# Computing only the chosen expert of each token, from lists in DRAM, in a two-layer decoder on one core

## The chip, the cores and the metric

One Trainium2 chip, one NeuronCore. The metric is the device time of one launch in microseconds (us), median of several runs. The engines are TensorE (PE: matmuls and transposes), VectorE (DVE), ScalarE (ACT), GpSimd (POOL) and SyncE (SP, which here only issues transfers). Each runs its own instruction list in order and waits on semaphores for the others.

## The reference

Two decoder layers on x of shape (16, 512, 256) in float32. Each sublayer is added to x after a layer norm. Layer 0 is a gated linear scan over the sequence, a cross attention with 16 heads on 64 context tokens, and a dense sublayer. Layer 1 is a positional attention whose parameters come from an LSTM over the sequence, a second cross attention, and this mixture of experts, the sublayer that the change is about:

```python
logits = jnp.einsum('bsd,ed->bse', x, w_router)          # 8 experts
indices = jnp.argmax(softmax(logits), axis=-1)
onehot = jax.nn.one_hot(indices, NUM_EXPERTS)
h = jnp.einsum('bsd,ehd->bseh', x, w_fc)                 # 256 -> 128 for each expert
h = jnp.where(h >= 0, h, 0.5 * h)
h = h * h
out = jnp.einsum('bseh,edh,bse->bsd', h, w_proj, onehot) # 128 -> 256
```

Each of the 8192 tokens uses one expert of eight.

## The kernel before

The work is cut into units of 128 positions of 4 sequences (512 tokens, `NT`): 4 chunks of positions by 4 groups of sequences, 16 units for each layer. A kernel-long schedule has six stages. Stages 0 and 1 run two units of layer 0 side by side in each body (2 bodies each; stage 1 has 64 LSTM steps in a body beside them). In stages 2 and 3 each of 4 bodies has one unit of layer 0, one of layer 1 (a chunk two behind) and 32 LSTM steps. In stage 4 a body has a unit of layer 1 and 32 LSTM steps, in stage 5 a unit of layer 1 alone.

The order of instructions on each engine is written by a planner at build time (`planned`). It lists the steps of each stream (`layer0_steps`, `layer1_steps`, `lstm_steps`) with a cost and what each needs, and places them one by one. LSTM steps have due times: in a body of stage 2, 3 or 4 the 32 of them are spread over 128, 140 or 112 of the planner's units (`PACE`). In stages 0, 4 and 5 (`WARM`) it fills nine tenths of each gap that it plans for PE with matmuls whose result nobody reads ("warm": bf16, 128x512), which keep PE busy. The planner decides the order alone; the real time of a step is the chip's.

An LSTM step is a loop over three engines: `gates` on PE, tanh on ACT, three small operations on DVE, tanh on ACT, the new state and its transpose on DVE, and then the next `gates`.

The expert part of a unit is computed densely. After the last norm, PE computes the router's 512x8 logits (`router` 0), DVE and ACT find each token's expert, PE turns the one-hot (`router` 4), and then for each of the 8 experts: `hidden` on PE (two 128x128 by 128x512 matmuls), ReLU on ACT, `leaky` on DVE, `select` on PE (spreads the one-hot of this expert over partitions), `kept` on DVE (multiplies by it), Square on ACT, and `expert` on PE (four 128x128 by 128x256 matmuls that add into two PSUM banks). `x6` adds the sum to the residual and SP stores the unit to `out`. The weights of all experts (`wfc`, `wpj`) are loaded once at the start.

## Time and profile before

| | us |
|---|---|
| median of 3 runs | 3078.72 (3077.14 to 3085.44) |
| profiled execution, its own time | 3086.61 |
| its span, first to last instruction | 3084.7 |
| PE busy | 2724.8 (88%) |
| DVE busy | 2042.3 (66%) |
| POOL busy | 1045.9 (34%) |
| ACT busy | 932.5 (30%) |

In the span, the share of busy time of an engine is a mean over stages with different limits. The store of a unit to `out` marks the end of each layer-1 unit. By these stores the stages take: start and stages 0 and 1 708 us, stage 2 683, stage 3 687, stage 4 529, stage 5 473. "Interval" below is the time between two such stores. In the profile an fp32 matmul counts as two instructions. PE's granted clock (PEclk) is a mean share of full speed. The trace names the DRAM copies of x and its norm `x_dram` and `xln_dram`.

### The profile page before, as it was taken

How to read it: one execution, taken by the hardware profiler on the slowest of the kernel's cores; microseconds unless marked ns; L12 is line 12 of the kernel's file. 1: busy time of each engine (PE TensorE's matmuls, PEld its weight loads, DVE VectorE, ACT ScalarE, POOL GpSimd, SP SyncE). 2: the span in 40 equal slices, each digit the busy share in tenths (PEclk: the TensorE clock that was granted, in tenths of full speed). 3: DMA queues.
4: the chain of work that ended last, by engine and by line, in shares of the span. 5: the costliest groups of instructions: out<-in, count | busy, mean ns of one | idle time of the engine just before them, and what ended most of it. 6: DMA issues, size and time to landing. Idle time of an engine off the chain costs nothing.

```text
span 3084.7 us, 38068 instructions
## 1 busy us (share of the span) xinstructions
PE 2724.8 (88%) x11733; PEld 1591.8 (52%) x11733; DVE 2042.3 (66%) x6490; ACT 932.5 (30%) x2361; POOL 1045.9 (34%) x956
## 2 busy tenths in 40 slices
PE   5799897886888988897988889898999998999999
PEld 2465554352555555463645555554555554555555
DVE  3576776887878696867778696866475664434433
ACT  0133233242324233332423233332322332222222
POOL 0254432332525242513425242513141340422422
PEclk9899897897899899888888999998999998999999
DMA  5210201001010101101010101000011010110100
GB/s 173 68 50 14 64 1 50 1 28 60 15 52 15 53 14 39 35 12 48 26 48 14 59 14 38 22 27 28 29 34 34 14 35 28 42 41 16 53 27 8
DMA packets 127166, 110.37 MB, mean 36 GB/s; under 512 B 31234, under 2 KB 126039, under 8 KB 126624
## 3 DMA queue, kind: packets, MB, share of 16 engines
q1 hardware_dynamic: 127008, 108.55, 11.4%
q8 instruction: 64, 1.05, 0.1%
q14 instruction: 94, 0.77, 0.1%
HBM read 76.81 MB, written 31.72 MB: 35 GB/s over the span
## 4 chain that ended last, share of the span: by engine, by line
PE 40%; issue 26%; DVE 23%; POOL 8%; ACT 2%; SPq 1%; DMA 1%; POOLq 0%; DVEq 0%; ACTq 0%
PE p L687 4%; PE p L781 4%; PE p L842 4%; PE p L854 4%; PE p L744 4%; PE p L720 3%; DVE l_xnat L1049 3%; DVE uin L1278 3%; PE p L681 3%; PE p L698 3%; PE pg L753 2%; PE p L734 2%; POOL l_scratch L1360 2%; DVE ln_stats L1024 2%; DVE l_scratch L1075 2%
## 5 line engine op out<-in xcount | busy, mean ns | idle before, releaser
L1348 POOL TENSOR_TENSOR l_kbd<-l_kg,headmask 128x512 f32<-128x512 f32 x256 | 265.4, 1047 | 376.7 <-PE p L720 277.4
L1334 POOL TENSOR_TENSOR ln_rstd<-ln_ve,neghalf 128x4 f32<-128x4 f32 x96 | 97.9, 1020 | 863.5 <-DVE ln_ve L1033 862.9
L1278 DVE SCALAR_TENSOR_TENSOR uin<-gates 16x20 f32<-16x20 f32 x512 | 185.7, 363 | 215.2 <-ACT gates L879 212.3
L1355 POOL TENSOR_TENSOR l_scratch<-l_scratch,l_mx 128x512 f32<-128x512 f32 x256 | 266.7, 1046 | 148.7 <-DVE l_mx L1079 147.9
L744 PEld LDWEIGHTS p<-l_vg,l_scratch 128*128 128x128 f32 x2048 | 266.1, 202 | 95.8 <-DVE l_xnat L1092 37.9
L879 ACT ACTIVATE gates<-pg 16x80 f32<-16x80 f32 x512 | 115.2, 225 | 650.7 <-PE pg L753 649.5
L720 PE MATMUL p<-l_kbd,l_qT 128*128 128x512 f32 x512 | 282.9, 642 | 22.5 <-DVE l_scratch L1075 21.8
L744 PE MATMUL p<-l_vg,l_scratch 128*128 128x34 f32 x2048 | 278.2, 285 | 17.7 <-DVE l_xnat L1092 9.5
L761 PE MATMUL p<-warm 128*128 128x512 bf16 x1077 | 286.8, 395 | 0.0
L842 PE MATMUL p<-l_xT,wfc 128*128 128x512 f32 x512 | 283.4, 647 | 1.1 <-DVE hr L1232 1.0
L854 PE MATMUL p<-wpj,hq 128*128 128x256 f32 x1024 | 264.9, 387 | 8.5 <-ACT hq L955 8.5
L681 PE MATMUL p<-ident,l_xnat 128*128 128x128 f32 x1024 | 188.1, 316 | 86.8 <-DVE l_xnat L1049 84.8
L753 PE MATMUL pg<-wcat,slots 128*16 128x80 f32 x1024 | 170.6, 252 | 93.6 <-DVE slots L1290 91.6
L854 PEld LDWEIGHTS p<-wpj,hq 128*128 128x128 f32 x1024 | 187.0, 190 | 91.1 <-issue 59.2
L753 PEld LDWEIGHTS pg<-wcat,slots 128*16 128x16 f32 x1024 | 58.1, 96 | 335.6 <-DVE slots L1290 167.4
L681 PEld LDWEIGHTS p<-ident,l_xnat 128*128 128x128 f32 x1024 | 133.8, 160 | 167.2 <-DVE l_xnat L1049 127.8
L1075 DVE TENSOR_TENSOR l_scratch<-p,l_neg 128x512 f32<-128x512 f32 x256 | 174.4, 683 | 49.0 <-PE p L720 43.9
L908 ACT ACTIVATE l_scratch<-p 128x512 f32<-128x512 f32 x256 | 149.4, 591 | 136.5 <-PE p L734 135.4
L890 ACT ACTIVATE l_xT<-p 128x512 f32<-128x512 f32 x192 | 105.6, 593 | 269.9 <-PE p L681 269.1
L734 PE MATMUL p<-ident,l_scratch 128*128 128x128 f32 x1024 | 169.2, 294 | 17.7 <-POOL l_scratch L1360 6.1
L882 ACT ACTIVATE pg<-pg 16x20 f32<-16x20 f32 x512 | 72.3, 141 | 371.4 <-DVE pg L1281 369.6
L903 ACT ACTIVATE l_scratch<-l_scratch 128x512 f32<-128x512 f32 x256 | 159.1, 622 | 76.2 <-POOL l_scratch L1355 75.6
(166 smaller groups left out, 4762.4 us busy)
## 6 DMA issues: line engine op xcount, KB each, us to landing
xln<-xln_dram SPq DMA_DIRECT2D x40, 512.0 KB, 3.9
l_vg<-v_dram SPq DMA_DIRECT2D x32, 544.0 KB, 3.9
l_kg<-k_dram SPq DMA_DIRECT2D x32, 256.0 KB, 4.2
xln_dram<-l_xnat SPq DMA_DIRECT2D x16, 512.0 KB, 3.0
x_dram<-l_xres SPq DMA_DIRECT2D x16, 512.0 KB, 4.1
l_xres<-x_dram SPq DMA_DIRECT2D x16, 512.0 KB, 3.7
out<-l_xres SPq DMA_DIRECT2D x16, 512.0 KB, 2.9
xin<-in_x SPq DMA_DIRECT2D x12, 512.0 KB, 3.8
```

Of the source, the lines that this page charges most:

```text
L681: i = pe.transpose(banks[l][m][:, b * P:(b + 1) * P], src[:, b, m * P:(m + 1) * P], ident[:, :])
L720: pe.matmul(banks[l][j], w.qT[:, j, b * P:(b + 1) * P], w.kbd[b % 2][:, j, :, :].rearrange("p a k -> p (a k)"), start=True, stop=True).the ...
L734: i = pe.transpose(t_bank[l][:, p * P:(p + 1) * P], src, ident[:, :])
L744: i = pe.matmul(o_bank[l][:, q * VW:(q + 1) * VW], w.exT[:, j, p, :], w.vg[:, b, q * VW:(q + 1) * VW], start=True, stop=True)
L753: pe.matmul(pg[0:B, 0:80], slots[:, s % STEPS, :], wcat[:, :], start=True, stop=True).then_inc(l_pe, 1)
L761: pe.matmul(pg[:, :] if layer == 0 else banks[0][0], warm[:, 0:P], warm[:, :], start=True, stop=True)
L842: i = pe.matmul(banks[1][2 + i_ % 2], wfc[:, k, i_ * P:(i_ + 1) * P], tiles[1].xT[:, k, :], start=(k == 0), stop=(k == NH - 1))
L854: i = pe.matmul(pairs[1][:, b * D:(b + 1) * D], hq[i_ % 2][:, b * P:(b + 1) * P], wpj[:, i_, :], start=(i_ == 0 and b % 2 == 0), stop=(i_ ...
L1075: dve.tensor_tensor(w.ex[b % 2][:, heads, :], banks[l][j].rearrange("p (a k) -> p a k", a=NE), w.neg[:, b:b + 1, :].broadcast_to([P, NE, S ...
L1278: dve.scalar_tensor_tensor(uin[:, :], gates[:, 0:20], 1.0, gates[:, 60:80], ALU.add, ALU.mult)
L1348: pool.tensor_tensor(w.kbd[b % 2][:, j, :, :], w.kg[:, j, b:b + 1, :].broadcast_to([P, NE, SK]), headmask[:, :].rearrange("p (a o) -> p a ...
L1355: pool.tensor_tensor(ex, ex, w.mx[:, i_ % 4, :].rearrange("p (a o) -> p a o", o=1).broadcast_to([P, NE, SK]), ALU.subtract).then_inc(t.shi ...
```

## The change

The dense expert part goes from the units of layer 1. Instead:

- Each unit ends with `router`, a `rank` on PE (six small bf16 matmuls that give every token its place in its expert's list: tokens before it in its tile, in the unit's other tiles and in earlier units), a `slot` on DVE (six small operations) and `ids` on POOL (four indexed DMAs of 128 rows of 8 bytes, which write the tokens' numbers into `id_dram`). The unit's residual and its norm are stored side by side in `x5_dram` (two DMAs of 512 KB), after the norm and no longer after the experts.
- Stage 5's first three bodies each also compute 20 tiles of 128 listed tokens, from the lists of chunks 0 to 2; a new stage 6 computes 24 more, of chunk 3 and with no other stream beside them. That is 84 tiles, whatever the routing is: the lists are padded with numbers out of bounds, which the DMAs skip.
- A tile: SP reads two numbers from SBUF (which expert, where its list goes on) and loads the list, the expert's two weights and so 128 KB twice; POOL gathers 128 rows of 2 KB with an indexed DMA; PE turns the norm (two transposes), ACT lands it, PE multiplies (`mhidden`), ACT, DVE and ACT do ReLU, the leaky sum and the square, PE multiplies again (`mexpert`), DVE adds the residual (`madd`), and POOL scatters 128 rows of 1 KB to `out` with an indexed DMA. There are four slots for tiles: the load of tile k waits for `mexpert` of tile k-4 and until its scatter has landed.
- `totals`, before stage 5 and before stage 6, counts the lists: one matmul and eleven small operations on DVE on one partition.
- `wfc` and `wpj` are no longer loaded (2 MB), and the start has some small operations on DVE and two stores of the empty list. `PACE` of stages 2 to 5 and the filling rule are as they were.

The diff, cut to its core:

```diff
-        return 5 * n + (0, 2, 3, 4)[k] if layer == 0 else 5 * self.first + 2 * n + k - 4
+        return 5 * n + (0, 2, 3, 4)[k] if layer == 0 else 5 * self.first + 3 * n + k - 4
...
+T = NC_ * B * P
+EARLY = 3
+TILE_SLOTS = 4
+TILES = (20, 24)
...
+    steps += [("sp", "store", 0, 0.1, [("norm", 11)])]
     steps += [("pe", "router", 0, 2.4, [("land", 11)]), ("dve", "router", 1, 0.4, [("router", 0)]),
               ("act", "router", 2, 0.15, [("router", 1)]), ("dve", "router", 3, 0.5, [("router", 2)]),
-              ("pe", "router", 4, 0.5, [("router", 3)]), ("act", "router", 5, 0.5, [("router", 4)])]
-    for e in range(NE):
+              ("pe", "rank", 0, 0.4, [("router", 3)]), ("dve", "slot", 0, 1.4, [("rank", 0)]), ("pool", "ids", 0, 4.0, [("slot", 0)])]
+def expert_steps(count, every):
+    for k in range(count):
         steps += [
-            ("pe", "hidden", e, 1.7, [("router", 5), ("kept", e - 2)]),
-            ...
-            ("pe", "expert", e, 1.75, [("squared", e)])]
+            ("clock", "due", k, every, [("due", k - 1)]),
+            ("sp", "mload", k, 1.5, [("due", k - 1), ("mexpert", k - TILE_SLOTS), ("mscatter", k - TILE_SLOTS)]),
+            ("dma", "mids", k, 0.1, [("mload", k)]),
+            ("pool", "mgather", k, 1.3, [("mids", k), ("madd", k - TILE_SLOTS)]),
+            ("dma", "mrows", k, 0.1, [("mgather", k)]),
+            ("pe", "mturn", k, 0.25, [("mrows", k), ("mland", k - 1)]),
+            ...
+            ("dve", "madd", k, 0.42, [("mexpert", k), ("mscatter", k - 2)]),
+            ("pool", "mscatter", k, 1.3, [("madd", k)])]
...
+    if stage == NC_ + 1 and ahead:
+        streams[3] = expert_steps(TILES[0], TILE_EVERY)
+    elif stage == NC_ + 2:
+        streams[3] = expert_steps(TILES[1], 0.5)
...
+            def load_expert(q):
+                s = q % TILE_SLOTS
+                if q >= TILE_SLOTS:
+                    sp.wait_ge(m_expert, q - TILE_SLOTS + 1)
+                    sp.wait_ge(o_store[q % 2], 16 * ((q - TILE_SLOTS) // 2 + 1))
+                ...
+                which = sp.value_load(tile_i[0:1, 0, j:j + 1], min_val=0, max_val=NE - 1)
+                start = sp.value_load(tile_i[0:1, 1, j:j + 1], min_val=0, max_val=ID_ROWS - P)
+                sp.dma_start(xid[s][:, :], id_dram[bass.ds(start, P), :]).then_inc(m_in[s], 16)
+                sp.dma_start(xw[s][:, 0:D]..., halves(a["w_fc"])[:, :, bass.ds(which * P, P)]).then_inc(m_in[s], 16)
+                sp.dma_start(xw[s][:, D:2 * D], a["w_proj"][:, bass.ds(which, 1), :]...).then_inc(m_in[s], 16)
...
+                elif family == "slot":
+                    dve.tensor_tensor(place[:, :, :], qb[:, 0:GB * NE]..., chosen[:, :, :], ALU.mult)
+                    ...
+                    dve.tensor_copy(slot_i[:, :], slot_f[:, :]).then_inc(rank_small, 1)
...
+                elif family == "ids":
+                    pool.wait_ge(rank_small, 5 * n + 5)
+                    for b in range(GB):
+                        pool.indirect_dma_start(id_dram, bass.IndirectOffsetOnAxis(ap=slot_i[:, b:b + 1], axis=0), tok[:, b, :],
+                                                None).then_inc(ids_store, 16)
...
+            def pool_expert(family, k, r, j):
+                if family == "mgather":
+                    if positive(q - TILE_SLOTS + 1):
+                        pool.wait_ge(m_added, q - TILE_SLOTS + 1)
+                    pool.wait_ge(m_in[s], 48 * turns + 48)
+                    pool.tensor_tensor(held[:, 1 + s:2 + s], neghalf[0:1, 0:1], neghalf[0:1, 1:2], ALU.mult).then_inc(m_take, 1)
+                    ...
+                    pool.indirect_dma_start(xg[s][:, :], None, rows5[0:stored], bass.IndirectOffsetOnAxis(ap=xid[s][:, 0:1], axis=0),
+                                            bounds_check=stored - 1, oob_is_err=False).then_inc(m_rows[s], 16)
+                else:
+                    pool.wait_ge(m_added, q + 1)
+                    ...
+                    pool.indirect_dma_start(rows6, bass.IndirectOffsetOnAxis(ap=xid[s][:, 1:2], axis=0), xy[k % 2][:, :], None,
+                                            bounds_check=T - 1, oob_is_err=False).then_inc(o_store[k % 2], 16)
```

How the order of instructions moves, at three places. First, PE in stage 4's loop body, before, behind the turn of the one-hot (L834; `wcat,slots` is an LSTM step, `wfc` is `hidden`, `sel` is `select`):

```order
L834 MATMUL p<-ident,lg 8x128 x4
L752 REGISTER_ALU
L753 MATMUL pg<-wcat,slots 16x80
L761 MATMUL p<-warm 128x512 x2
L842 MATMUL p<-l_xT,wfc 128x512 x3
L751 REGISTER_ALU
L752 REGISTER_ALU
L753 MATMUL pg<-wcat,slots 16x80
L842 MATMUL p<-l_xT,wfc 128x512
L848 MATMUL p<-ohT,sel 128x512
```

And after the change, behind the last matmul of `rank` (L932):

```order
L932 MATMUL p<-first,every 128x32
L840 REGISTER_ALU
L841 MATMUL pg<-wcat,slots 16x80
L849 MATMUL p<-warm 128x512 x13
L839 REGISTER_ALU
L840 REGISTER_ALU
L841 MATMUL pg<-wcat,slots 16x80
L849 MATMUL p<-warm 128x512 x13
```

The dense experts are gone from between the LSTM steps, and 13 filling matmuls stand between each step and the next: eight such groups (104 matmuls) in a loop body of stage 4, with nine LSTM steps. In all PE has 229 filling matmuls in such a body where it had 135; in stage 5's first three bodies 214 where it had 135, 118 of them behind `rank`; and in its last body 123 where it had 133, none of them behind `rank`.

Second, PE at the end of a body of stage 3, before (`wpj` is `expert`, `wih` the LSTM's input gates, L800 the next unit's rows):

```order
L848 MATMUL p<-ohT,sel 128x512
L753 MATMUL pg<-wcat,slots 16x80
L854 MATMUL p<-wpj,hq 128x256 x2
L681 MATMUL p<-ident,l_xnat 128x128 x4
L854 MATMUL p<-wpj,hq 128x256 x2
L681 MATMUL p<-ident,l_xnat 128x128 x4
L854 MATMUL p<-wpj,hq 128x256 x4
L753 MATMUL pg<-wcat,slots 16x80
L794 MATMUL p<-l_xT,wih 96x512 x2
L800 MATMUL p<-R,wms 128x512
```

And after, from `rank` on:

```order
L927 MATMUL p<-chosen,before 128x32
L928 MATMUL p<-counts,every 128x32
L930 MATMUL p<-chosen,every 128x24
L930 MATMUL p<-chosen,every 128x16
L930 MATMUL p<-chosen,every 128x8
L932 MATMUL p<-first,every 128x32
L769 MATMUL p<-ident,l_xnat 128x128 x4
L841 MATMUL pg<-wcat,slots 16x80
L769 MATMUL p<-ident,l_xnat 128x128 x4
L882 MATMUL p<-l_xT,wih 96x512 x2
L841 MATMUL pg<-wcat,slots 16x80 x6
L888 MATMUL p<-R,wms 128x512
```

Six LSTM steps stand in a row at the end, with nothing of another stream between them; at the end of a body of stage 2 two do. The rest of the body's LSTM steps and layer-0 steps stand in front of `rank`.

Third, POOL at the end of a body of stage 5, before (L1305 and L1334 belong to the last norm, L1348 and L1370 are the next unit's keys and squared weights):

```order
L1305 TENSOR_TENSOR l_xres<-l_xres,rowO 128x1024
L1333 REGISTER_ALU
L1334 TENSOR_TENSOR ln_rstd<-ln_ve,neghalf 128x4
L377 REGISTER_ALU
L377 COMPARE_AND_BRANCH
L1348 TENSOR_TENSOR l_kbd<-l_kg,headmask 128x512 x2
L1370 TENSOR_TENSOR wsq<-wT 128x512
```

And after (`held` is a one-element operation that passes on a wait, `out<-xy` a scatter):

```order
L1586 TENSOR_TENSOR held<-neghalf 1x1
L1587 DMA out<-xy,xid 8192x256
L1585 REGISTER_ALU
L1586 TENSOR_TENSOR held<-neghalf 1x1
L1587 DMA out<-xy,xid 8192x256
L1585 REGISTER_ALU
L1586 TENSOR_TENSOR held<-neghalf 1x1
L1587 DMA out<-xy,xid 8192x256
L414 REGISTER_ALU
L414 COMPARE_AND_BRANCH
L1535 TENSOR_TENSOR l_kbd<-l_kg,headmask 128x512 x2
L1566 TENSOR_TENSOR wsq<-wT 128x512
```

Behind `rank` such a body now has the gathers of 10 tiles and the scatters of 12, and the next unit's first instructions on POOL stand behind the last scatter, of tile 19. The loads of these tiles stand on SP in the same way in front of the next unit's loads.

## Rows read from the trace of the kernel before

**Rows 1.** Windows by interval, stages 0, 2, 3, 4, 5: window, length, busy us (instructions), clock, DMA.

```profile
core 0: us, PE busy (x) PEld busy (x) DVE busy (x) ACT busy (x) POOL busy (x), PEclk, DMA share, GB/s
224.40:347.00 122.60, 120.71 (x559) 75.92 (x558) 85.35 (x243) 40.16 (x70) 55.00 (x46) 1.00 0.13 40
1059.60:1223.80 164.20, 146.11 (x612) 87.77 (x612) 128.41 (x400) 56.63 (x145) 64.11 (x58) 0.91 0.10 31
1748.00:1917.60 169.60, 147.74 (x632) 89.14 (x630) 129.12 (x400) 56.55 (x147) 64.78 (x59) 0.92 0.11 33
2354.20:2481.30 127.10, 119.20 (x540) 65.04 (x540) 79.20 (x279) 38.21 (x114) 37.20 (x36) 0.99 0.10 29
2852.00:2970.50 118.50, 114.80 (x495) 66.35 (x494) 49.87 (x115) 29.92 (x52) 36.69 (x33) 0.96 0.12 36
```

**Rows 2.** Lines, whole kernel: line, engine, operation, tiles, count, busy us, mean ns, idle before.

```profile
L842 PE MATMUL p<-l_xT,wfc 128*128 128x512 f32 x512 | 283.4, 647 | 1.1 <-DVE hr L1232 1.0
...
L854 PE MATMUL p<-wpj,hq 128*128 128x256 f32 x1024 | 264.9, 387 | 8.5 <-ACT hq L955 8.5
...
L1232 DVE TENSOR_TENSOR hr<-p,hr 128x512 f32<-128x512 f32 x128 | 88.3, 690 | 96.2 <-PE p L848 95.3
...
L1227 DVE TENSOR_TENSOR hr<-p,hr 128x512 f32<-128x512 f32 x128 | 88.0, 687 | 91.4 <-ACT hr L950 90.3
...
L950 ACT ACTIVATE hr<-p 128x512 f32<-128x512 f32 x128 | 76.3, 596 | 171.0 <-PE p L842 170.9
...
L1317 POOL COPY slots<-R 96x128 f32<-96x128 f32 (+1 forms) x64 | 24.8, 396 | 33.6 <-ACT R L926 33.6
...
L1328 POOL TENSOR_TENSOR nrm<-nrm,neghalf 128x4 f32<-128x4 f32 x16 | 16.2, 1012 | 59.6 <-DVE nrm L1196 59.6
```

**Rows 3.** Windows inside intervals: stages 2, 2 and 3, then expert parts of stages 4 and 5.

```profile
1080.20:1162.60 82.40, 73.39 (x332) 43.15 (x330) 74.58 (x223) 31.96 (x81) 39.77 (x37) 0.97 0.05 13
1172.90:1214.10 41.20, 40.94 (x157) 24.46 (x157) 22.52 (x85) 13.72 (x37) 3.37 (x2) 0.94 0.07 21
1769.20:1854.00 84.80, 73.25 (x332) 42.65 (x331) 77.15 (x218) 30.83 (x78) 43.82 (x42) 0.96 0.08 25
2441.90:2479.90 38.00, 38.00 (x138) 19.84 (x137) 18.40 (x66) 13.15 (x35) 0.00 (x0) 1.00 0.00 0
2932.40:2970.50 38.10, 38.10 (x126) 20.59 (x125) 12.01 (x19) 10.29 (x18) 0.00 (x0) 0.96 0.00 0
```

**Rows 4.** Timeline of PE in stage 4: start us, us, engine, line, operation, tiles, count, idle before.

```profile
2373.02 0.31 PE L753 MATMUL pg<-wcat,slots 128*16 128x80 f32 x2
2373.27 2.98 PE L761 MATMUL p<-warm 128*128 128x512 bf16 x13
2376.33 0.31 PE L753 MATMUL pg<-wcat,slots 128*16 128x80 f32 x2
...
2386.26 0.31 PE L753 MATMUL pg<-wcat,slots 128*16 128x80 f32 x2 [0.26 <-DVE slots L1290]
...
2388.41 0.31 PE L753 MATMUL pg<-wcat,slots 128*16 128x80 f32 x2
```

**Rows 5.** Timeline of the DMA queue: one unit's context loads, and the last store.

```profile
1839.85 0.36 SPq L580 DMA_DIRECT2D l_vg<-v_dram  x1
...
1840.83 0.60 SPq L586 DMA_DIRECT2D mask<-in_mask  x1
...
3081.11 0.38 SPq L611 DMA_DIRECT2D out<-l_xres  x1
```

**Rows 6.** DMA issues by tile: queue, count, KB each, median us to landing.

```profile
l_kg<-k_dram SPq DMA_DIRECT2D x32, 256.0 KB, 4.2
out<-l_xres SPq DMA_DIRECT2D x16, 512.0 KB, 2.9
...
v_dram<-l_vg SPq DMA_DIRECT2D x32, 136.0 KB, 1.7
```

**Rows 7.** Window over the weight loads at the start, columns as in Rows 1.

```profile
5.00:38.00 33.00, 5.18 (x8) 2.67 (x9) 11.05 (x29) 0.00 (x0) 0.00 (x0) 1.00 0.73 237
```

More of the change, by code:

```diff
@@ L22 @@
 BF16 = mybir.dt.bfloat16
+I32 = mybir.dt.int32
 AX_X = mybir.AxisListType.X
@@ L324, in planned @@
         waiting.remove(key)
-        order.append((engine, *key))
+        if engine not in ("dma", "clock"):
+            order.append((engine, *key))
     kept, last = [], 0.0
@@ L337, in planned, with run_stages @@
     return kept
-PLANS = {(stage, ahead): planned(stage, ahead) for stage in range(NC_ + 2) for ahead in (False, True)
-         if stage >= 2 or not ahead}
+PLANS = {(stage, ahead): planned(stage, ahead) for stage in range(NC_ + 3) for ahead in (False, True)
+         if 2 <= stage < NC_ + 2 or not ahead}
 def positions(c, g):
     return sum(range(1, c + 1)) * NG + (c + 1) * g
-def run_stages(engine, name, step, lstm_step):
+def run_stages(engine, name, step, lstm_step, expert_step, totals):
     def body(stage, r, ahead=False):
@@ L358, in body @@
                 step(0, stage, family, index, 0, 0, 0, 0)
+            elif who == name and stream == 3:
+                expert_step(family, index, r if stage == NC_ + 1 else EARLY - 1, index if stage == NC_ + 1 else TILES[0] + index)
             elif who == name:
@@ L370, in run_stages @@
     for stage in range(2, NC_ + 2):
+        if stage == NC_ + 1:
+            totals(0)
         for who, index in (("pe", 0), ("act", 1), ("dve", 2), ("dve", 3)):
@@ L374, in run_stages @@
                 step(1, layer, "rows", index, c, g, n, m)
-        if stage == 2:
+        unrolled = stage in (2, NC_ + 1)
+        if unrolled:
             body(stage, 0, ahead=True)
-        with engine.Fori(1 if stage == 2 else 0, NG - 1) as r:
+        with engine.Fori(1 if unrolled else 0, NG - 1) as r:
             body(stage, r, ahead=True)
         body(stage, NG - 1)
+    totals(1)
+    body(NC_ + 2, 0)
 def decoder_program(nc, a, out):
@@ L405, in decoder_program @@
         neghalf = sb("neghalf", [P, GB])
-        sel = sb("sel", [NE, NE, P], BF16)
+        ones_row = sb("ones_row", [1, NE])
+        held = sb("held", [1, 8])
+        before = sb("before", [P, P], BF16)
+        every = sb("every", [P, P], BF16)
+        first = [sb(f"first{i}", [P, NE], BF16) for i in range(2)]
+        counts = sb("counts", [P, NE], BF16)
         posl = sb("posl", [64, NC_, P])
@@ L550, in _ @@
                 sp.dma_start(dst, src).then_inc(w_load, 16)
+            for i in range(2):
+                sp.dma_start(id_dram.rearrange("(i p n) o -> i p (n o)", i=2, p=P)[i], nobody).then_inc(k_store, 16)
             sp.wait_ge(prep_ev, 8)
@@ L759, in pe_step @@
                 elif family == "warm":
-                    pe.matmul(pg[:, :] if layer == 0 else banks[0][0], warm[:, 0:P], warm[:, :], start=True, stop=True)
+                    pe.matmul(banks[0][0] if layer == 4 else pg[:, :], warm[:, 0:P], warm[:, :], start=True, stop=True)
                 elif family == "turn":
@@ L859, in _ @@
-            run_stages(pe, "pe", pe_step, pe_lstm)
+                    if positive(n):
+                        pe.wait_ge(counts_done, n)
+                    phase = 0 if c < EARLY else 1
+                    ranks = qb[:, 0:GB * NE].rearrange("p (b e) -> p b e", b=GB)
+                    spread = lambda v: v.rearrange("p (o e) -> p o e", o=1).broadcast_to([P, GB, NE])
+                    pe.matmul(ranks, before[:, :], chosen[:, :, :], start=True, stop=False, skip_group_check=True)
+                    pe.matmul(ranks, every[:, :], spread(counts[:, :]), start=False, stop=False, skip_group_check=True)
@@ new lines, in pe_step, with pe_totals @@
+                    for b in range(GB - 1):
+                        pe.matmul(ranks[:, b + 1:GB, :], every[:, :], chosen[:, b:b + 1, :].broadcast_to([P, GB - 1 - b, NE]),
+                                  start=False, stop=False, skip_group_check=True)
+                    pe.matmul(ranks, every[:, :], spread(first[phase][:, :]), start=False, stop=True,
+                              skip_group_check=True).then_inc(rank_pe, 1)
+            def pe_totals(phase):
+                pe.wait_ge(counts_done, NG * (EARLY if phase == 0 else NC_) + phase)
+                pe.matmul(banks[0][0][:, 0:NE], every[:, :], counts[:, :], start=True, stop=True).then_inc(rank_pe, 1)
@@ L985, in _ @@
             dve.tensor_scalar(wOut[:, :, :], wOut[:, :, :], 0.25, None, ALU.mult)
-            dve.tensor_copy(sel[:, :, :], sel32)
+            dve.tensor_tensor(before[:, :], tri[:, :], ident[:, :], ALU.subtract)
+            for i in range(2):
+                dve.tensor_scalar(first[i][:, :], rank[:, :], -float(ROOM[i]), float(BASE[i] + NE * ROOM[i]), ALU.mult, ALU.add)
+            for i in range(2):
+                dve.tensor_scalar(steps_row[:, i, :], jrow[:, 0, 0:64], float(S * (1, P)[i]), -float((1, P)[i]), ALU.mult, ALU.add)
             dve.tensor_scalar(biasA[:, :], biasA[:, :], 0.5, None, ALU.mult)
```

330 lines of the change are left out of this document (223 added, 107 removed).

## The prediction

> **What bounds the kernel now.** I read the page's busy table first (PE 88%, DVE 66%), then the windows of one interval of each stage, since the shares are means over stages with different limits. In [rows 1] the reader is to see two regimes. In stages 2 and 3 an interval takes 164 and 170 us, with PE busy for 146 and 148 and DVE for 128 and 129. In stages 4 and 5 it takes 127 and 118.5 us, with PE at 119 and 115 and DVE at 79 and 50; but there PE's busy time holds about 135 filling matmuls, which no result needs. Then the windows inside an interval [rows 3]: before the experts DVE is the fuller engine (74.6 of 82.4 us, 77.2 of 84.8: 0.905 and 0.91), and in the expert part PE is full (40.9 of 41.2, 38.0 of 38.0, 38.1 of 38.1) with DVE at half or less. So the expert part is a stretch of some 38 us bound by PE, which each of the 16 units adds in front of its store. The lines confirm the size: `hidden` 283.4 and `expert` 264.9 us are 34.3 us of PE for a unit, and `leaky` and `kept` 88 us each are 11.0 of DVE [rows 2]; `x6` adds two DVE operations of the same form, 1.4.
>
> The change takes that stretch away everywhere. What stands in its place differs by stage, and the order shows it, so I price four pieces apart. Times are against the profiled execution.
>
> **The start: -6.** 2 MB less is loaded; at 237 GB/s [rows 7] that is 8.8 us on the path, since PE, ACT and DVE all start on the last load. Some fifteen new small DVE operations stand behind it, 2 to 3 us, of which part is hidden while DVE waits for PE. Bounds: -9 to +2. The stores of the empty list are early and small.
>
> **Stages 2 and 3, eight intervals: -240.** DVE becomes the bound. In stage 2 it keeps 128.4 - 12.4 and gets `slot`, six operations of about 0.18 us each: 117.1. PE keeps about 107, POOL gets four indexed DMAs on its 64 us. At the density of [rows 3], 0.905, that is 129.4 us, and two LSTM steps stand alone at the end (a step alone takes 2.15 us [rows 4]; half of that is added, since its DVE work is counted already): 131.6, 32.6 less. In stage 3, 129.1 - 12.4 + 1.1 = 117.8, by 0.91 is 129.5, and six lone steps add 6.4: 135.9, 33.7 less. The beginnings and ends of an interval are less dense than those windows, so I take 30 for each. The bounds are 38 (all of the stretch and no more: the new DVE bound can't gain more than the PE bound gave) and 15 (rival B). `ids` waits for `slot`, and behind it on POOL stand the next unit's keys and squared weights; POOL is busy for 64 of 164 us there [rows 1], so it is hidden; were it not, it would cost its four DMAs, some 5 us a unit.
>
> **Stage 4, four intervals: -40.** Here the gain is mostly filled up again. Behind `rank` the order has eight groups of one LSTM step and 13 filling matmuls. The same group stands in the trace: from 2373.02 to 2376.33, 3.31 us [rows 4]. Eight are 26.5, with `rank` and the ninth step 28, where the experts took 38.0 [rows 3]. So 10 an interval. LSTM steps alone could run at 2.15, so without the filling it would be 19; the filling sets the pace. Bounds: 5 to 15.
>
> **Stage 5: +28.** This and the tail hang on one number, the period P of a tile. The load of tile k waits until tile k-4 is scattered, so P is a quarter of this loop:
> - SP: two reads of a number, which no row shows (0 to 3, I take 1.5), and three DMA issues, 1.5 from the first to the end of the third in [rows 5];
> - landing of the loads. In [rows 6] 136 KB stored take 1.7, 512 KB stored 2.9, 256 KB loaded behind another load 4.2: I take 2.8, and the same for the gather (256 KB) and the scatter (128 KB);
> - on POOL, for gather and scatter alike, `held` (the nearest is the small copy, 0.4) and the writing of 128 descriptors, which no row shows. The nearest is POOL's small operation at 1.01 [rows 2]. I take 1.3 together, between 0.4 and 2.4;
> - the arithmetic: a turn, a landing, two matmuls, ReLU, sum, square, a matmul, an addition. The nearest rows are 0.39 a matmul record, 0.60 an ACT and 0.69 a DVE operation for forms two to four times as wide [rows 2]; with seven handovers I take 4.5, between 3.3 and 5.5.
>
> 3.0 + 2.8 + 1.3 + 2.8 + 4.5 + 1.3 + 2.8 = 18.5, a quarter is 4.6, and with queues in order on five engines P = 4.8. The lower ends give 2.7, the upper ones 6.9.
>
> The page "DMA: Bandwidth & Descriptors" of the Trainium skill (section on the anatomy of a DMA on the gpsimd path) prices a DMA at about 2.0 us plus bytes by 436 GB/s. The rows don't quite agree: 512 KB would be 3.2, and the trace has 2.9 for the store. By that rule gather and scatter would land in 2.6 and 2.3, P would be 4.6 and the forecast 2935.
>
> In each of the first three bodies the gathers of ten tiles stand behind `rank`, and the last scatter in front of the next unit's work on POOL. That is eleven periods, 53 us, where the experts took 38.1: +15; before `rank` the queues of POOL and PE wait now and then for a tile that isn't there yet, +5. So +20 for each, +60. PE does not bound it: 118 filling matmuls at 2.98 us for 13 [rows 4] are 27, and 12 tiles at some 1.3 (three fp32 matmuls at two records of 0.2 to 0.39 each [rows 2], and a turn) are 16. `totals` is eleven DVE operations in a row at the start of the stage: +5. The last body has neither experts nor tiles behind `rank`: 38.1 - 1.5, so -37. Sum +28.
>
> **The tail: +121.** `totals` and the first load, 6; then 24 tiles, 115. Nothing runs beside them. Before, the kernel ended with the last store at 3081.1 [rows 5].
>
> **The sum.** 3084.7 - 6 - 240 - 40 + 28 + 121 = 2948 us of span. The profiled execution took 3086.6, 1.9 more than its span, and the median of the runs is 7.9 below that: 2942. I say 2945. A microsecond of P is worth 24 + 33 = 57 us.
>
> **Rivals.** A: the tile loop decides, and the kernel is slower. The place is POOL and the four slots, the price P. 2945 + 57 (P - 4.8) passes 3088 at P = 7.3. That needs, for instance, 4 us on POOL for an indexed DMA: two are then 8 a tile, and P = 8 gives 3127. For it: no row shows an indexed DMA, and 128 rows each want a descriptor. Against it: all the upper ends together give only 6.9.
>
> B: stages 2 and 3 do not shrink so far, since the streams' own chains decide. Two units of layer 0 side by side, with no LSTM and no layer 1, already take 122.6 us [rows 1], with PE full in part by filling; with LSTM steps between, an interval of 150 is possible. That is 15 saved where I take 30: 3065. Against it: [rows 3] has DVE, not waits, as the full engine in front of the experts.
>
> C: the tiles flow better: P = 3.7, and intervals of 129 and 132: 2945 - 63 - 30 = 2852.
>
> D: descriptors of the indexed DMAs are held up by DVE. DVE is at 0.9 in the dense parts of stages 2 and 3 [rows 3]; a wait of one 0.7 us operation for each of the two DMAs of a tile is 0.35 on P for the 33 periods of stage 5, and nothing in the tail, where DVE is nearly idle: +12, with some `ids` later, 2960. The page "SBUF — State Buffer" of the Trainium skill (SBUF: two separate sides) warns that a GpSimd DMA cannot write its descriptors while DVE runs a two-port operation, 3.1 us in place of 0.62; no row here shows such a DMA. At 2.5 us each time it would be 1.2 on P, and 2985.
>
> That the change doesn't save what it says is not open: 84 tiles are done whatever the routing, 10752 places for 8192 tokens, and the eightfold work is gone.
>
> **Chances.** My forecast 0.60 (2890 to 3010), C 0.13, A 0.12, B 0.10, D 0.05. A measurement of this kernel tells 0.3% from no change, 3069 to 3088. Faster: 0.60 + 0.13 + 0.05, and half of B: 0.83; the other half of B and a little of A is same, 0.06; slower 0.11. The range takes in C and most of B, and of A only P up to 6.8: 2850 to 3060.
>
> **What would show it.** Intervals of about 132 and 136 us in stages 2 and 3 with DVE at nine tenths, and PE near 107. In stage 4 intervals near 117, with 3.3 us from `gates` to `gates` behind `rank`. In stage 5 three bodies near 138 with POOL waiting for tile loads, one near 74. In the tail a period near 4.8 from gather to gather, on a chain of DMA landings, with PE nearly idle. An indexed DMA over 3 us on POOL, or stages 2 and 3 with DVE well under 0.85, would make it wrong.

## The result

| | median us (runs) | lowest to highest | profiled: span, mean granted clock |
|---|---|---|---|
| before | 3080.9 (4) | 3077.1 to 3085.4 | 3084.7, 0.919 |
| after | 3192.0 (4) | 3175.9 to 3192.8 | 3189.5, 0.847 |

The ratio is 1.0347, 95% interval 1.0311 to 1.0384: the changed kernel is slower, where I had forecast 2945 us and a range up to 3060. Span against span it is 104.8 us more, 241.5 more than the sum of the prediction (2948). Both profiled executions, cut at the stages' ends:

| piece | predicted | measured | error |
|---|---|---|---|
| start | -6 | -6.5 | 0 |
| stages 2 and 3, eight intervals | -240 | -100.3 (1366.2 to 1265.9) | +140 |
| stage 4 | -40 | -40.4 (534.5 to 494.1) | 0 |
| stage 5 | +28 | +111.9 (472.9 to 584.8) | +84 |
| tail | +121 | +140.2 (3.6 to 143.8) | +19 |

The lengths come from the stores of layer 0 in the DMA queue (stages 2 and 3), and from PE's `totals` matmuls at 2460.92 and 3045.73, where stage 5 and the tail begin; before, from the stores to `out` at 2608.18 and at 3081.11 [rows 5].

### The profile page after: what moved, and what is told of

Its sections match the earlier page's. It is cut to its first block, busy times and chain, and to the rows that moved or that the text cites. A ratio compares the mean times of both kernels' runs of the same rounds, so it can differ in the third digit from the quotient of the medians.

```text
span 3189.5 us, 39732 instructions
## 1 busy us (share of the span) xinstructions
PE 2584.9 (81%) x11385; PEld 1542.6 (48%) x11385; DVE 1893.2 (59%) x6517; ACT 853.2 (27%) x2341; POOL 1317.4 (41%) x1372
## 3 DMA queue, kind: packets, MB, share of 16 engines
q1 hardware_dynamic: 182352, 137.55, 14.6%
## 4 chain that ended last, share of the span: by engine, by line
PE 36%; issue 21%; DVE 19%; POOL 12%; DMA 6%; SPq 3%; ACT 2%; POOLq 0%; DVEq 0%; ACTq 0%
PE p L775 4%; PE p L869 4%; PE p L832 4%; PE p L808 4%; PE p L769 3%; DVE l_xnat L1185 3%; PE p L786 3%; DMA out<-xy,xid 3%; DMA xw<-in_w_proj 3%; PE p L822 2%; POOL l_scratch L1547 2%; PE pg L841 2%; DVE ln_stats L1160 2%; PE p L849 2%; POOL l_scratch L1542 2%
## 5 line engine op out<-in xcount | busy, mean ns | idle before, releaser
L1465 DVE SCALAR_TENSOR_TENSOR uin<-gates 16x20 f32<-16x20 f32 x512 | 175.5, 343 | 283.4 <-ACT gates L987 281.5
L832 PEld LDWEIGHTS p<-l_vg,l_scratch 128*128 128x128 f32 x2048 | 282.2, 215 | 75.0 <-issue 36.6
L832 PE MATMUL p<-l_vg,l_scratch 128*128 128x34 f32 x2048 | 292.7, 296 | 15.9 <-ACT l_scratch L1016 6.8
L769 PE MATMUL p<-ident,l_xnat 128*128 128x128 f32 x1024 | 202.0, 339 | 123.2 <-DVE l_xnat L1185 122.0
L849 PE MATMUL pg<-warm 128*128 128x512 bf16 x905 | 245.1, 400 | 1.3 <-DVE l_sums L1155 1.3
L769 PEld LDWEIGHTS p<-ident,l_xnat 128*128 128x128 f32 x1024 | 146.8, 173 | 189.4 <-DVE l_xnat L1185 160.2
L849 PE MATMUL p<-warm 128*128 128x512 bf16 x922 | 228.0, 384 | 0.0
L1547 POOL TENSOR_TENSOR l_scratch<-l_scratch,gp 128x512 f32<-128x512 f32 x128 | 162.0, 1268 | 34.6 <-DVE l_sums L1218 34.1
L1215 DVE TENSOR_REDUCE l_mx<-l_scratch 128x8 f32<-128x512 f32 x256 | 171.4, 674 | 4.5
L822 PEld LDWEIGHTS p<-ident,l_scratch 128*128 128x128 f32 x1024 | 133.4, 160 | 71.9 <-issue 47.8
```

The lines of the kernel that those rows point to most:

```text
L769: i = pe.transpose(banks[l][m][:, b * P:(b + 1) * P], src[:, b, m * P:(m + 1) * P], ident[:, :])
L822: i = pe.transpose(t_bank[l][:, p * P:(p + 1) * P], src, ident[:, :])
L832: i = pe.matmul(o_bank[l][:, q * VW:(q + 1) * VW], w.exT[:, j, p, :], w.vg[:, b, q * VW:(q + 1) * VW], start=True, stop=True)
L849: pe.matmul(banks[0][0] if layer == 4 else pg[:, :], warm[:, 0:P], warm[:, :], start=True, stop=True)
L1215: dve.tensor_reduce(w.mx[:, u % 4, :], w.ex[b % 2][:, heads, :], AX_X, ALU.max).then_inc(t.top, 1)
L1465: dve.scalar_tensor_tensor(uin[:, :], gates[:, 0:20], 1.0, gates[:, 60:80], ALU.add, ALU.mult)
```

## The profile after

First the windows by interval, as in [rows 1] and with its columns: one interval of stage 2, 3 and 4 of the changed kernel, then the tail from `totals` to the first gather, from there to the last gather, and the rest.

```profile
1191.20:1344.90 153.70, 128.90 (x510) 83.56 (x509) 102.89 (x372) 45.93 (x125) 66.12 (x60) 0.74 0.13 41
1502.10:1658.80 156.70, 125.59 (x530) 77.81 (x528) 114.52 (x387) 47.09 (x129) 68.96 (x65) 0.80 0.13 39
2195.20:2315.90 120.70, 113.41 (x533) 59.99 (x533) 67.47 (x266) 28.25 (x96) 41.42 (x41) 0.93 0.12 35
3045.70:3062.40 16.70, 0.18 (x1) 0.10 (x1) 2.64 (x13) 0.00 (x0) 4.40 (x6) 0.61 0.07 16
3062.40:3175.90 113.50, 59.27 (x176) 38.93 (x176) 14.86 (x43) 20.40 (x67) 52.17 (x86) 0.50 0.38 109
3175.90:3189.50 13.60, 5.91 (x16) 3.74 (x16) 1.86 (x5) 1.84 (x7) 5.81 (x9) 0.50 0.01 0
```

DVE's busy time in stage 3 fell to 114.5 us, near what I had (117.8), but it fills 0.73 of the interval, not 0.91. PE was busy for 125.6 us where I had 107, and is still the fuller engine of the two. The granted clock fell from 0.91 and 0.92 [rows 1] to 0.74 and 0.80: a larger part of these intervals runs at 1.2 GHz, and the matmuls there take longer. The four records of the LSTM's input gates, at the start of an interval (columns as in [rows 2]), before and then after:

```profile
L794 PE MATMUL p<-l_xT,wih 128*96 128x512 f32 x4 | 1.9, 592 | 0.0
```

```profile
L882 PE MATMUL p<-l_xT,wih 128*96 128x512 f32 x4 | 3.7, 1088 | 1.2 <-ACT l_xT L998 1.2
```

Where the interval went shows in the DMA queue. Its rows (start us, us, line, what is issued) are layer 0's store at the end of a unit, the load of the next input, which waits until DVE has the next unit's first norm behind it, and the next store. First the kernel before, then the changed one, both in stage 3:

```profile
1568.71 0.37 SPq L607 DMA_DIRECT2D xln_dram<-l_xnat  x1
...
1591.23 0.37 SPq L569 DMA_DIRECT2D xin<-in_x  x1
...
1740.39 0.37 SPq L607 DMA_DIRECT2D xln_dram<-l_xnat  x1
```

```profile
1502.09 0.36 SPq L672 DMA_DIRECT2D xln_dram<-l_xnat  x1
...
1535.83 0.37 SPq L634 DMA_DIRECT2D xin<-in_x  x1
...
1658.76 0.36 SPq L672 DMA_DIRECT2D xln_dram<-l_xnat  x1
```

I call the first stretch the head and the second the rest: 22.5 + 149.2 us before, 33.7 + 123.0 after. The rest gave 26 us and the head took 11 back. In stage 2 the same cut gives 15.5 + 148.7 before and 25.1 + 130.5 after. The windows of both parts, as above, before and then after:

```profile
1568.70:1591.20 22.50, 16.00 (x56) 9.69 (x54) 16.12 (x55) 6.02 (x16) 8.71 (x7) 0.77 0.29 95
1591.20:1740.40 149.20, 136.34 (x577) 83.36 (x577) 112.37 (x345) 50.57 (x130) 56.06 (x52) 0.91 0.08 24
```

```profile
1502.10:1535.80 33.70, 17.89 (x50) 7.97 (x48) 18.38 (x77) 7.20 (x25) 14.30 (x14) 0.55 0.16 48
1535.80:1658.80 123.00, 107.70 (x481) 69.84 (x480) 96.15 (x311) 39.89 (x104) 54.66 (x51) 0.87 0.12 37
```

In the rest DVE is busy for 0.78 of the time (96.15 of 123.0), where it had been 0.75 before (112.37 of 149.2); at 0.91 the rest would take 106 us. The density that the prediction used is there for some 60 us of it, and PE is hardly less busy in them:

```profile
1555.00:1615.00 60.00, 52.66 (x232) 29.93 (x232) 54.50 (x156) 24.31 (x61) 32.92 (x31) 0.94 0.00 0
```

In the head after the change PE and DVE are each busy for about 18 of 33.7 us, at a clock of 0.55. PE's timeline there (columns as in [rows 4]) shows LSTM steps alone:

```profile
1510.38 0.45 PE L841 MATMUL pg<-wcat,slots 128*16 128x80 f32 x2 [1.72 <-DVE slots L1477]
1512.25 0.45 PE L841 MATMUL pg<-wcat,slots 128*16 128x80 f32 x2 [1.43 <-DVE slots L1477]
1514.12 0.45 PE L841 MATMUL pg<-wcat,slots 128*16 128x80 f32 x2 [1.42 <-DVE slots L1477]
```

They belong to the six steps that stand in a row (1508.21 to 1517.86), the last of the unit. Before, such steps ran beside the experts' matmuls; now every 1.87 us one of them stands in each queue ahead of the next unit's first norm.

Stage 5 is cut by the first matmul of `rank` (L927), PE's timeline again:

```profile
2572.35 0.19 PE L927 MATMUL p<-chosen,before 128*128 128x32 bf16 x1
...
2747.15 0.23 PE L927 MATMUL p<-chosen,before 128*128 128x32 bf16 x1
...
2906.01 0.19 PE L927 MATMUL p<-chosen,before 128*128 128x32 bf16 x1
...
3044.72 0.19 PE L927 MATMUL p<-chosen,before 128*128 128x32 bf16 x1
```

From rank to rank it takes 174.8, 158.9 and 138.7 us. The last scatter of the ten tiles behind each rank leaves POOL 76, 65 and 63 us after it (2648.4, 2811.8 and 2969.3), where I had 53. In front of a rank the stretch is then 99 and 94 us with ten tiles in it, and 75.4 without, at the end.

In the tail POOL gathers 24 tiles (POOL's timeline, same columns): first and last gather are 113.5 us apart, 4.93 a tile.

```profile
3061.72 0.18 POOL L1580 TENSOR_TENSOR held<-neghalf 1x1 f32<-1x1 f32 x1 [10.54 <-DMA xw<-in_w_proj]
3062.46 1.05 POOL L1582 DMA_INDIRECT xg<-x_dram,xid  x1 [0.56 <-issue]
...
3175.92 1.02 POOL L1582 DMA_INDIRECT xg<-x_dram,xid  x1 [0.51 <-issue]
```

The chain of waits (start us, us, what) shows the loop of a slot: scatter landing, SP's two reads and three issues, the load's landing, the gather.

```profile
3105.00 3.49 DMA out<-xy,xid
...
3108.86 0.15 SPq L708
...
3109.82 0.33 SPq L710
...
3110.91 2.87 DMA xw<-in_w_proj
...
3113.92 0.18 POOL held L1580
...
3114.61 1.01 POOL xg L1582
```

## The experiments: stages 2 and 3

Five kernels, each run once, ask what the missing experts left behind. The times of "head" and "rest" are those of the second and following intervals of stage 3.

**no_experts.** The kernel before without its experts and with nothing new:

```diff
-    for e in range(NE):
-        steps += [("pe", "hidden", e, ...), ..., ("pe", "expert", e, ...)]
-    steps += [("dve", "x6", h, 0.65, ...) for h in range(2)]
-    steps += [("sp", "store", 0, 0.1, [("x6", 1)])]
+    steps += [("sp", "store", 0, 0.1, [("router", 5)])]
```

> The kernel before without its eight experts: behind the router the unit's x5 is stored as it is, so the experts' sum is missing from the output, and nothing of the change's new work is there (no rank, no slots, no indexed DMA, one store of 512 KB in place of two). Read are the intervals of stages 2 and 3, 164 and 170 us before, 154 and 156 after the change. If the new work costs what is missing (theory N: POOL's indexed DMAs and the two stores stand on the path), they fall to the 132 and 136 us that I had predicted. If the streams' own orders and chains set the interval once the experts are gone (theory O: the LSTM steps are still handed out over 128 and 140 us of plan, and run alone at the end, with PE at 1.2 GHz), they stay at 150 to 156, as after the change.

The intervals of stage 3 took 163, 160, 160 and 151 us (head 34.4, rest 126), the eight together 1249 against 1266 after the change. The same eight intervals took 1252 to 1266 us in the four profiled kernels whose instructions there are those of the change (after, slots10, slots10_order4, no_late_ids), so all that the change adds costs 3 to 17 us in stages 2 and 3, and the taking out alone brings 117 of my 240. It does not add up by stage: without the new work stage 2 took 614 us and not 630 to 644, but stage 3 635 and not 622, and that is left open. Theory O held for the sum, N fell. This is rival B's interval of 150 us.

**no_ids.** The changed kernel without the list writes:

```diff
-                    for b in range(GB):
-                        pool.indirect_dma_start(id_dram, ...).then_inc(ids_store, 16)
```

> The changed kernel without the four indexed DMAs per unit that write the token lists (the lists stay empty, so no token's expert is added in stage 5 and the tail; these two are not read, or only for what a gather without rows costs). Intervals of stages 2 and 3. Theory N: POOL is held for 4 x 1.26 = 5 us in front of the reciprocal root that the next norm waits for, so an interval falls by about 5 us, 40 us in all eight. Theory O: POOL's DMAs lie beside lone LSTM steps, an interval falls by under 2 us.

Stage 3 took 157.9, 157.2, 157.1 and 149.8 us, against 157.2, 156.7, 157.0 and 151.1, and the eight intervals together 1264 against 1266: nothing. That `ids` are hidden there, as I had it, holds, though POOL does stand in front of a root with them.

**pace.** Other due times, nothing else:

```diff
-PACE = {... 2: (128.0, 4.0, 0.3), 3: (140.0, 0.0, 0.4), 4: (112.0, -18.0, 0.35),
+PACE = {... 2: (112.0, 4.0, 0.3), 3: (114.0, 0.0, 0.4), 4: (90.0, -18.0, 0.35),
```

> The changed kernel with other due times of the LSTM steps: they are handed out over 112, 114 and 90 us of plan in stages 2, 3 and 4 in place of 128, 140 and 112, so that no run of lone steps stands at the end of a unit. Nothing else is changed. Theory O: intervals fall from 154 and 156 to about 138 in stages 2 and 3, and from 117 to about 100 in stage 4, 200 us in all twelve. Theory N or C: under 5 us an interval in stages 2 and 3. Should the LSTM steps get in the way of the dense middle, the intervals do not fall at all, since DVE is at 0.93 there.

It took 3137 us in one run, 55 less, not 200. The DMA queue of stage 3:

```profile
1514.01 0.36 SPq L672 DMA_DIRECT2D xln_dram<-l_xnat  x1
...
1534.22 0.37 SPq L634 DMA_DIRECT2D xin<-in_x  x1
...
1664.81 0.36 SPq L672 DMA_DIRECT2D xln_dram<-l_xnat  x1
```

The head fell by 13.5 us to 20.2: the lone steps had made it. But the rest grew by 7.5 to 130.6, where the steps now are, and stage 2 lost 15 us of the 21 that stage 3 won: the eight take 1260.4 us, and 1253 to 1260 in the four kernels below with these due times. Nearly all of the gain, 46 us, is in stage 4, whose last groups of a step and 13 fillings (28.4 us behind the last rank after the change) are gone. So due times decide where the steps wait, not much how long the interval is.

**ballast.** Work that nobody reads, on PE:

```diff
+              *[("pe", "ballast", k, 2.0, [("rank", 0)]) for k in range(8 if c < 2 else 0)],
...
+                    for _ in range(9):
+                        pe.matmul(qc[:, :], warm[:, 0:P], warm[:, :], start=True, stop=True)
```

> The changed kernel with 72 matmuls of bfloat16 (128 x 512, no one reads them) behind the rank of every unit of stages 2 and 3, 16 us of PE at the full clock, where before the experts' matmuls stood. Theory C, the clock: the granted clock at the end of an interval and in the 33 us after it, 0.5 to 0.54 now, rises to near 1, the layer-0 products there take half as long, and the interval stays at 154 us or falls by up to 8 in spite of 16 us more of PE. Theory O without a share of the clock: the matmuls fill gaps between LSTM steps and delay them, the interval grows by 3 to 16 us.

The intervals of stage 3 grew to 167 us. The rest grew by 17, about what the matmuls take, and the head fell by 6, with the clock there at 0.69 in place of 0.55. The clock is not all of these 6 us, since four lone LSTM steps stand in this head and not six; that is 3.7 us. The input gates took 1.9 us in place of 3.7, and a lone step 1.73 in place of 1.87:

```profile
1526.22 0.31 PE L842 MATMUL pg<-wcat,slots 128*16 128x80 f32 x2
1527.95 0.31 PE L842 MATMUL pg<-wcat,slots 128*16 128x80 f32 x2 [1.42 <-DVE slots L1481]
```

So the lower clock costs some 2 us in a head of stage 3 (an estimate from these rows). In stage 2 the four intervals took 648 us with the matmuls and 644 without: 64 us more work for PE cost 4, at a clock of 0.83 to 0.86 in place of 0.74 to 0.84. There PE had room, or the higher clock paid for the matmuls; this run does not separate the two, and theory C, which had the interval stay, is refuted for stage 3 alone.

**dve_extra.** The same on DVE:

```diff
+    steps += [("dve", "extra", k, 1.4, [("gate", k)]) for k in range(8 if c < 2 else 0)]
...
+                    for i in range(2):
+                        dve.tensor_tensor(xg[(2 * i_ + i) % 4][:, :]..., two(rowOut), two(rowF), ALU.add)
```

> The changed kernel with sixteen more DVE additions (128 x 512, no one reads them) in each unit of stages 2 and 3, in the attention's dense part, about 11 us of DVE. If DVE bounds the interval, as my sum had it (theory D), the part of an interval behind its head grows by 11 us or more, 88 in all eight intervals. If the streams' chains and the slow clock bound it (theory O), DVE's idle quarter takes most of them in, and an interval grows by under 6 us.

The group of lines over one interval, columns as in [rows 2]:

```profile
L1363 DVE TENSOR_TENSOR xg<-rowOut,rowF 128x512 f32<-128x512 f32 x16 | 12.9, 844 | 0.1
```

For these 12.9 us the rest of the three stage-3 intervals grew by 9.4 on the mean (122.7 to 132.1), in stage 2 by 2.6 (an interval there by 1.7), and the head not at all. That lies between the two theories: theory O fell for stage 3 (9.4 is over its 6), and theory D's 11 was not reached. Behind the head of stage 3 more work lengthens the interval by most of itself, on DVE (9.4 for 12.9) as on PE (17 for some 16, in ballast), although neither engine is full over that stretch (0.78 and 0.88). That the two bound it in turn is argued from this, not shown by itself. In stage 2 neither costs much. Over an interval DVE was busy 0.78 and 0.76 before [rows 1], 0.67 and 0.73 after.

## The experiments: stage 5 and the tail

| kernel | us (runs) | stage 5 | tail | period in the tail |
|---|---|---|---|---|
| after | 3192 (4) | 584.8 | 143.8 | 4.93 |
| slots10_order4 | 3107 (1) | 537 | 125.5 | 4.10 |
| slots10 | 3065 (1) | 492.6 | 113.1 | 3.36 |
| both | 3024 (4) | 509 | 116.3 | 3.43 |
| xy4 | 3006 (4) | 482 | 113.8 | 3.48 |

The first column is a median where there are four runs, the others are from one profiled execution each. How far these agree: both, warmtail and mid have the same stage 5 and took 509, 500 and 501 us there; the tails of both, mid and nofill5, which are the same too, took 116.3, 111.8 and 112.1. So a difference under some 10 us in stage 5, or under 5 in the tail, shows nothing.

**slots10.** Ten slots; layer 0's buffers serve for six, and semaphores of the start are used again:

```diff
-TILE_SLOTS = 4
+TILE_SLOTS = 10
-        xw = [sb(f"xw{i}", [P, 2 * D]) for i in range(TILE_SLOTS)]
+        xw = [sb(f"xw{i}", [P, 2 * D]) for i in range(4)] + [idle.scratch[:, 2 * D * i:2 * D * i + 2 * D] for i in range(6)]
```

> The changed kernel with ten tile slots in place of four (six of them in buffers of layer 0, which is done by then), so that a load waits for the scatter of tile k-10. Stages 0 to 4 are as before, 2427 us. Theory S (the slots' loop of about 20 us sets the period): P falls from 4.9 to what SP needs for a tile, 2.8 us, or POOL's two indexed DMAs, 2.8; the tail goes from 144 to about 95, and a stage-5 body of 162 to 171 us to about 140, 130 us in all. Theory Q (the queues in order: fill and drain of the pipeline at the rank and the next unit set stage 5, and one tile's latency of 18 us is paid at each end): the tail falls as in S, but a body of stage 5 by less than 10 us.

3065 us, 127 less: theory S. SP's waits in the tail (line waited for, us, times, longest), after the change and then here:

```profile
SPq L705 <- DMA out<-xy,xid: 48.3, 10, 8.3
```

```profile
SPq L710 <- DMA out<-xy,xid: 3.0, 5, 1.6
```

The stage won 92 us and the tail 31, in place of 49: the period is 3.36, not 2.8.

**slots10_order4.** Ten slots, queues in the order made for four:

```diff
-[("due", k - 1), ("mexpert", k - TILE_SLOTS), ("mscatter", k - TILE_SLOTS)]
+[("due", k - 1), ("mexpert", k - PLANNED_SLOTS), ("mscatter", k - PLANNED_SLOTS)]
```

> Ten slots for the tiles, but the order of the instructions as the planner makes it for four (with ten it also puts 17 gathers of a body in front of the rank in place of 9). Ten slots with their own order took the stage-5 bodies from 171 and 162 us to 140 and the tail from 144 to 107. Theory S (the loop of a slot sets the period): nearly all of that stays, bodies at 140 to 147, kernel at 3065 to 3085. Theory R (the order did it in stage 5, the tail has only tiles and is the same in both): bodies at 155 or more, tail near 107, kernel at 3110 or more.

3107 us, between the two. In stage 5 the slots themselves make 48 us and the order 44; in the tail 18 and 12 (the tail of slots10 is 113.1, not the 107 of the expectation). Here theory R was wrong too: the tail's queues differ in order as well.

**both.** slots10 with the due times of pace.

> Ten slots and the earlier due times of the LSTM steps together. The due times alone gave 3137 us. By theory S 3005 us and faster than the kernel before (3081); by theory Q 3085, no difference from it.

3024.1 us, ratio to before 0.9803 (0.9754 to 0.9851), between what S and Q had given: faster than the kernel before, though it isn't certain that it is by 2%.

**warmtail.** The same, with fillings in the tail:

```diff
-IDLE, FILL, WARM = 0.3, 0.9, (0, 4, 5)
+IDLE, FILL, WARM = 0.3, 0.9, (0, 4, 5, 6)
```

> The same as the one with ten slots and earlier due times, and in the tail filling matmuls (128 x 512, bfloat16) in PE's planned gaps, as stages 0, 4 and 5 have them. The tail's PE ran at 1.2 GHz, with PE 65 us busy. If the clock matters where a tile's chain is waited for, its PE steps halve, 1.5 us of 18 a tile: the tail falls by 2 to 8 us. If SP or POOL sets the period, nothing changes; if the fillings delay tiles, it is up to 15 us longer.

3026.7 us, 0.9833 (0.9790 to 0.9877), no difference from both. The tail took 113.0 us at a clock of 0.82, and without fillings 111.8 to 116.3: no gain from the clock shows.

**nofill5.** The same as both, `WARM = (0, 4)`:

> Ten slots and the earlier due times, without the filling matmuls of stage 5. With them this kernel took 3024 us, and each of the three long bodies has some 117 fillings, 27 us of PE at the full clock. If they stand in the way of the tiles, a body is up to 10 us shorter and the kernel at 2995 to 3015. If they keep the clock up for the attention, a body is longer by 5 to 15 us, 3040 to 3070.

3044.1 us, 0.9896 (0.9860 to 0.9931). The fillings are not in the way of the tiles. Whether they help is open: the median is 20 us higher than that of both, but stage 5 took 511 us in the profiled execution (the fastest of its four), against 509 in that of both (the slowest of its four).

**mid.** Ten slots, `PACE` 120, 126 and 82:

> Ten slots, with the LSTM steps handed out over 120, 126 and 82 us of plan in stages 2, 3 and 4 (112, 114 and 90 gave 3024 us, 128, 140 and 112 gave 3065). The earlier due times took the head of a stage-3 interval from 34 to 20 us and added 7.5 to the rest. If the two trade one for one, nothing between them is better, and stages 2 and 3 stay within 10 us; if a few lone steps cost nothing, up to 25 us are won there. Stage 4 should fall from 109 to some 105 an interval, 12 to 16 us in all.

3036.0 us, 0.9865 (0.9831 to 0.9899). Stages 2 and 3 took 1264 us, against 1260 and 1266: head and rest trade. Stage 4 took 454 us against 445 in both, so the 12 to 16 us hoped for there did not come either.

**xy4.** both, with four result buffers. In the trace of both, DVE waited for them in the second body of stage 5 (2527 to 2674 us):

```profile
DVE xy L1428 <- DMA out<-xy,xid: 28.6, 7, 10.9
```

```diff
-        xy = [sb(f"xy{i}", [P, D]) for i in range(2)]
+        xy = [sb(f"xy{i}", [P, D]) for i in range(4)]
-                    dve.wait_ge(o_store[k % 2], 16 * halved)
+                    dve.wait_ge(o_store[k % 4], 16 * turns)
```

> Ten slots and the earlier due times (3024 us), and four buffers for a tile's result in place of two. In the trace of that kernel DVE's addition waits 35 us of the tail for the scatter of the tile before the last to land, 14 times, and a tile takes 3.43 us from gather to gather. Theory X (the pair of result buffers is the loop that ten slots left): addition, issue and landing, some 6 us, are then shared by four tiles, and the period falls to SP's 2.8: 24 x 0.6 = 14 us less in the tail and as much in stage 5, 2995 us. Theory Y (SP's reads and issues and POOL's two indexed DMAs, 2.8 us each, with their jitter, set it): under 8 us in all.

3005.8 us, 0.9746 (0.9730 to 0.9763): 2.5% faster than the kernel before, and the fastest here that computes everything. Theory X held in stage 5 (482 us against 500 to 509; DVE's waits for a landing scatter, 61 us there in both, are no longer in the trace, though 25 us of waits without a named source are). It fell in the tail, whose period stayed, though these waits fell from 47 us to 9. What sets 3.4 us there, over SP's 2.8, is open.

**no_late_ids.** The changed kernel, with the list writes left out of the last chunk:

```diff
-                    for b in range(GB):
+                    for b in range(GB if c < EARLY else 0):
                         pool.indirect_dma_start(id_dram, ...
```

> The changed kernel without the indexed DMAs of the four units of the last chunk (four per unit, 128 rows of 8 bytes each): the last chunk's tokens then stand in no list, and the tail's 24 tiles gather no rows and are not read, only the wait in front of them. Read are the three stretches of stage 5 from the rank to the last scatter of the ten tiles behind it, 76, 65 and 63 us after the change where I had predicted 53, and the 16.7 us from the tail's totals to its first gather, where I had predicted 6. Theory I (the lists' writes stand in front of the tiles on POOL, 5.3 us, and on the DMA rings): each stretch falls by 5 us or more, the first by up to 16, since its scatter took 13.3 us to land and a load 13.9 right behind these DMAs; the tail's first gather comes about 9 us sooner. Theory F (filling and draining four slots make the rest): the stretches stay within 2 us.

The stretches behind the rank were 67, 70 and 65 us, against 76, 65 and 63, and the tail's first gather came 8.6 us after `totals`, not 16.7. So in the bodies the list writes are not it, but for some 9 us in the first; the second grew by 5, which neither theory has. That filling and draining the slots is the rest (theory F) is what remains, and slots10_order4, with the same order of instructions and ten slots, agrees with it: its stretches are 62, 55 and 52 us. At the tail's start the writes cost 8 us, since the first load waits for their landing (theory I).

## Why the prediction was wrong

**Start, stage 4: right.** Both within 1 us. The mechanism of stage 4 is the one I had: behind its last rank stand 28.4 us at a clock of 1.00, for my 28, in groups of 3.15 us for my 3.31. That the sum agrees to 0.4 us is luck: the stage took 487 to 494 us in the four profiled kernels whose instructions there are those of the change.

**Stages 2 and 3: the step "DVE becomes the bound at the density of [rows 3]".** Those windows cover 82 of 164 us and are the densest, and in them PE is at 0.89 and 0.86 [rows 3], hardly behind DVE. After the change 0.91 is there for some 60 us of a stage-3 interval; over the interval it is 0.73. Against the 135.9 us of my sum that interval took 156.7: some 17 us more in the rest, at 0.78 and not 0.91, some 7 more in the head, less 4 since DVE had less to do. I had also left the clock at nothing: PE was busy for 125.6 us, not 107. So 12.5 us an interval were saved and not 30.

The head was longer by 6 to 11 us, since LSTM steps that had run beside the experts now stood alone in front of the next unit. I had priced this at 6.4 us for six steps, but in a window that did not contain the head. My 2.15 us for a step alone was misread as well: in [rows 4] a product of the query stands between the two steps, and PE is busy all the time. The line that the row leaves out:

```profile
2386.50 1.98 PE L698 MATMUL p<-l_xT,wQ 128*128 128x512 f32 x4
```

The row that would have warned was in [rows 1]: DVE busy 128.4 of 164.2 and 129.1 of 169.6. Those shares, 0.78 and 0.76, on my 117 give 150 and 155 us; measured were 153.7 to 171.3 and 151.1 to 157.2. That they come so near is partly luck, since after the change DVE had less work (102.9 and 114.5 us) at a lower share still. Rival B had the interval and got 0.10; its mechanism, chains and not a full engine, is what stage 2 shows, and in part what the rest of stage 3 shows. What sets a stage-2 interval was not found.

**Stage 5: the step "eleven periods behind the rank, +5 in front of it".** P was right (4.93 for 4.8), but a pipeline of four slots also has to fill and drain: 204 us in three stretches where I had 159. The first of the twelve scatters behind a rank starts 12.5, 9.2 and 12.8 us after it, the eleven periods then take 62.6, 54.5 and 49.5 us (I had 53), and the last scatter 1: most of the 45 is the wait in front of the first scatter. Tiles in front of a rank cost some 20 us a body (99 and 94 against 75), not 5. SP waits there for scatters, in the first such stretch for 49 of its 99 us:

```profile
SPq L705 <- DMA out<-xy,xid: 49.1, 4, 26.7
```

That these scatters are late because they stand in POOL's queue behind the attention's own steps is read from the order, not tested. And the first 111 us from `totals` to the first rank had been 90 in my sum. Together +45, +23 and +21; the last body was 5 us shorter than I had it.

**The tail: +19.** 10.7 at the start, of which the list writes are 8; 11.9 at the end, the 13.6 us of the last tile behind its gather, which 24 periods do not hold; less the 3.6 us of the last store, which I had left in the sum.

**The rivals.** A had the sign and half of the place: stage 5 and the tail took 123 us less with ten slots, but P stayed under 7.3, and a POOL indexed DMA takes 1.0 us, 1.5 with its issue. C fell. D fell as far as this kernel shows: none of its indexed DMAs took over 1.21 us of POOL, also while DVE was busy for 0.67 to 0.73 of an interval (with ten slots a few gathers took 1.5). The Trainium skill has 3.1 us on its page "SBUF — State Buffer" (SBUF: two separate sides) for a collision with a two-port operation of DVE; none of that length is seen here, and no row here says whether such an operation ran beside one. The gather landed in 3.5 us and the scatter in 2.6 (medians of 84). The rule on the page "DMA: Bandwidth & Descriptors" of the Trainium skill (section on the anatomy of a DMA on the gpsimd path) gave 2.6 and 2.3.

The sign was lost by two errors of one kind, 140 and 84 us. With the first alone the sum would come to 3088 us, no change; with the second alone to 3032. Each takes a rate from a stretch in steady state, DVE's density or the period of a tile, and leaves out the ends of the stretch.

## What to carry to other kernels

Work that is taken out of a full engine was also cover for what ran beside it: list what stood beside it, and price that alone, at the place where it then stands. Take the density for a forecast from the whole interval, and keep the dense window as the optimistic end. A loop over a few slots costs its period times the count plus one latency for each time it starts and stops; more slots were the first thing to try here (127 us), and the next ring of buffers, the results, came right behind (18 us by the medians).

## What the runs showed of the hardware

An LSTM step alone took 1.87 us at a granted clock of 0.50 and 1.73 at 1.00 (in ballast), and the difference is that of its two matmuls, 0.45 and 0.31 us: they are a small part of that chain. A list write, 128 rows of 8 bytes and four of them in a row for a unit, lands in 5.2 us on the median, twice a scatter of 128 KB (2.6), and once in 15.7; beside that one a gather took 14.6 us and a load 13.9, against 3.5 and 2.5 on the median.
